# A Flamingo block on one core: query and key stacks written from PSUM by column-repeated fp32r weights, and all later keys and values projected in the prologue

## The reference, cut to what matters

```python
for L in range(4):
    x = x + tanh(g_xattn[L]) * xattn[L](layernorm(x), ctx)
    x = x + tanh(g_ffn[L]) * ffn[L](layernorm(x))
# xattn[1]: q = n @ Wq.T + bq; k = ctx @ Wk.T + bk; v = ctx @ Wv.T + bv
#           softmax(q k^T / sqrt(8)) v per head, then @ Wo.T + bo
# xattn[2]: no biases, no scale; one key and value head of 8 features shared by all 16 heads;
#           only keys with |key - query| <= 32 (NEG elsewhere)
# xattn[3]: as 1, and where(mask == 0, -10000, scores) ahead of the softmax
```

## Time and profile before

| what | value |
|---|---|
| runs | 831.49, 822.17 and 829.42 us, median 829.42 |
| span of the profiled execution | 829.3 us |
| PE busy | 651.2 us, 79% |
| VectorE busy | 551.9 us, 67% |
| ScalarE busy | 365.6 us, 44% |
| GpSimd busy | 297.9 us, 36% |
| DMA queue, share of 16 engines | 17.2% |
| instructions | 12053 |
| shares of the chain of waits | PE 66%, DVE 17%, DMA 8%, ACT 4%, issue 3% |

### The profile page before, as it was taken

The page is one execution under the profiler, slowest core; times in us unless marked ns, Lnnn a source line. Parts: engine busy times, 40 slices in busy tenths (PEclk is TensorE's granted clock), DMA queues, the critical chain, the costliest instruction groups (busy, mean ns, idle before and its releaser), DMA issues.

```text
span 829.3 us, 12053 instructions
## 1 busy us (share of the span) xinstructions
PE 651.2 (79%) x3570; PEld 421.2 (51%) x3570; DVE 551.9 (67%) x1490; ACT 365.6 (44%) x642; POOL 297.9 (36%) x551
## 2 busy tenths in 40 slices
PE   4347699962898787982699976999994399975997
PEld 4235477741345465751255553677763044444675
DVE  2785788873675438874567436788886478835686
ACT  1102345421467423431166632677773055641575
POOL 2963246621221242630111141567662011102463
PEclk9776599985699757995599985899997589985799
DMA  7000011255100200155300100111135500000011
GB/s 254 0 1 0 0 30 48 48 59 65 21 4 3 64 1 10 49 66 60 38 3 3 29 0 1 32 40 39 44 53 63 63 3 3 3 26 0 21 44 39
DMA packets 25339, 27.55 MB, mean 33 GB/s; under 512 B 4483, under 2 KB 23750, under 8 KB 25286
## 3 DMA queue, kind: packets, MB, share of 16 engines
q1 hardware_dynamic: 25286, 26.90, 17.2%
HBM read 16.63 MB, written 0.52 MB: 21 GB/s over the span
## 4 chain that ended last, share of the span: by engine, by line
PE 66%; DVE 17%; DMA 8%; ACT 4%; issue 3%; SPq 1%; POOL 1%; DVEq 0%; ACTq 0%; POOLq 0%
PE PS L547 10%; PE PS L548 10%; PE PS L549 9%; PE PS L721 5%; PE PS L704 5%; PE PS L675 5%; DMA qst<-qp 5%; PE PS L569 4%; PE PS L701 4%; DVE xn L979 2%; DMA qst<-nmT 2%; PE PS L734 1%; PE PS L635 1%; PE PS L468 1%; PE PS L634 1%
## 5 line engine op out<-in xcount | busy, mean ns | idle before, releaser
L329 POOL TENSOR_TENSOR wpair<-ring,ones_col 128x128 fp32r<-128x128 f32 (+1 forms) x150 | 78.0, 520 | 161.4 <-PE PS L549 131.1
L916 ACT ACTIVATE pT<-PS 128x512 f32<-128x512 f32 x192 | 110.8, 598 | 45.0 <-PE PS L704 40.0
L1160 DVE TENSOR_TENSOR pT<-pT,PS 128x512 f32<-128x512 f32 x150 | 102.4, 684 | 38.3 <-ACT pT L847 31.2
L675 PE MATMUL PS<-kst,qst 96*128 96x256 bf16 x384 | 85.4, 311 | 42.7 <-DMA qst<-qp 37.3
L1166 DVE TENSOR_TENSOR hid_lo<-pT,hid_hi 128x512 fp32r<-128x512 f32 x150 | 110.6, 738 | 2.4 <-ACT hid_hi L854 1.4
L331 POOL TENSOR_TENSOR wpair<-ring,wpair 128x128 fp32r<-128x128 f32 (+1 forms) x150 | 104.3, 695 | 11.8
L854 ACT ACTIVATE hid_hi<-pT 128x512 fp32r<-128x512 f32 x150 | 93.5, 623 | 15.8 <-DVE pT L1160 15.3
L547 PE MATMUL PS<-hid_hi,wpair 128*128 128x512 f32 x150 | 87.3, 582 | 4.1 <-DVE hid_lo L1166 4.1
L547 PE MATMUL PS<-xhi,wpair 128*128 128x512 f32 x204 | 88.0, 431 | 1.9 <-DVE pT L1160 1.1
L548 PE MATMUL PS<-xlo,wpair 128*128 128x512 f32 x204 | 84.6, 415 | 0.0
L847 ACT ACTIVATE pT<-PS,ring 128x512 f32<-128x512 f32 x96 | 66.0, 690 | 42.0 <-PE PS L549 42.0
(11 more groups left out here) (210 smaller groups left out, 1171.0 us busy)
## 6 DMA issues: line engine op xcount, KB each, us to landing
ring<-in_mlp SPq DMA_DIRECT2D x48, 128.5 KB, 2.0
ring<-in_glu SPq DMA_DIRECT2D x27, 192.0 KB, 2.4
kst<-kp SPq DMA_DIRECT2D x36, 128.0 KB
qst<-qp SPq DMA_DIRECT2D x36, 128.0 KB
qst<-nmT SPq DMA_DIRECT2D x96, 3.0 KB
att_w<-in_att_w SPq DMA_DIRECT2D x4, 257.0 KB, 8.2
consts<-in_consts SPq DMA_DIRECT2D x1, 988.5 KB, 5.6
x_res<-in_x SPq DMA_DIRECT2D x1, 512.0 KB, 3.7
```

Source lines behind the costliest of these rows:

```text
L675: mm = pe.matmul(PS[:, v % 2, j * S:(j + 1) * S], qst[0:KROWS, h0 + j, b * S + q * P:b * S + (q + 1) * P], kst[0:KROWS, h0 + j, b * S:(b + ...
L916: act.activation(pT[:, w % 8, :], PS[:, 2 + w % 2, :], ACT.Exp, scale=sc).then_inc(A["p"], 1)
L1160: dve.tensor_tensor(hid[:, hf, :], src[:, hf, :], PS[:, 6 + hf, :], ALU.mult).then_inc(M["hid"], 1)
```

## The change

**The stacks.** Queries and keys are no longer split in three bf16 parts. The weights are repeated by column, so that one projection writes for four heads (32 rows each) the rows: the 8 features three times, and 8 rows more of which two are used. `stacked(w)` on the host makes them. A stack is now in fp32r with 24 rows for a head (`SROWS`), 26 with the two rows for the maximum (`MROWS`), and head h lies in rows 32 (h % 4) on and in group h // 4 (`HGRP` = 4 groups). The three blocks of 8 rows are to hold high, rest and high part; ACT copies with a sign or zero for each row (`take_queries`), and VectorE adds the rest where it belongs (`finish_queries`); for keys two ACT copies and a POOL addition (`complete_keys`). The score matmuls use 24 or 26 rows, a tile of 32 of the array's 128 rows. The mask matmul stays one over 128 rows, the value matmul stays one of 128 rows and 32-column tiles with 9 columns in place of 32 (`vall` has 9).

**Queries.** Four projections for each half, of three fp32r matmuls of 512 columns each; in layers 1 and 3 a fourth one with two rows (`ones2`, `brow`) adds the bias. Those of the second half lie inside the loop at p = 4, 5, 8 and 9 (`Q_AT`). No DMAs fill the stacks; those of `nmT` stay (two for four units, 8 partitions).

**Keys and values** of layers 1 to 3 are projected in the prologue in 23 chunks (`chunks`), split over four places by `KV_AT`: 4 behind layer 0's value projection, 4 behind the query transform, 9 behind the correlation, 6 at the end. Context and key weights are split in two fp32r parts there by ACT and POOL. `kst` exists for each layer. POOL's five memsets of the stacks and `split_keys` go. The mask's loads stand ahead of the experts' weights on SP.

**The maxima.** A unit's two score matmuls are now one head's two query tiles, and not two heads'. `split_maxima` makes two fp32r parts with two operations and not four; `turn_max` is two fp32 transposes and not one in bf16. `LAG` is 14.

The core of the diff:

```diff
-PAIRS = ((0, 0), (0, 1), (1, 0), (1, 1), (0, 2), (2, 0))
-QUERY_ORDER = sorted(enumerate(PAIRS), key=lambda pair: pair[1][0])
-KROWS = 96
-SROWS = KROWS + PARTS
+HGRP = 4
+SROWS = 3 * HD
+MROWS = SROWS + 2
...
-        LAG = 12
+        LAG = 14
         NU = B * H
+        Q_AT = (4, 5, 8, 9)
+        KV_AT = (4, 8, 14, 17)
...
+        chunks = ([("k", 1, hf, a) for hf in range(NHALF) for a in range(HGRP)] + [("v", 1, hf, 0) for hf in range(NHALF)]
+                  + [("k", 2, hf, 0) for hf in range(NHALF)] + [("v", 2, 0, 0)]
+                  + [("k", 3, hf, a) for hf in range(NHALF) for a in range(HGRP)] + [("v", 3, hf, 0) for hf in range(NHALF)])
...
-            def stack_keys(L):
-                if L == 1:
-                    sp.wait_ge(stacks_set, 7)
-                else:
-                    sp.wait_ge(at["p"], (L - 1) * NU)
-                for hf in range(NHALF):
-                    sp.wait_ge(at["kparts"], (L - 1) * adds["kparts"] + hf + 1)
-                    for n, (_, g) in enumerate(PAIRS):
-                        sp.dma_start(kst[n * HD:(n + 1) * HD, :, hf * HALF:(hf + 1) * HALF],
-                                     kp[:, g, hf * HALF:(hf + 1) * HALF]).then_inc(at_kst[L][hf], 16)
 
...
-                        sp.dma_start(qst[n * HD:(n + 1) * HD, :, hf * HALF:(hf + 1) * HALF],
-                                     qp[:, g, hf * HALF:(hf + 1) * HALF]).then_inc(at_qst[L][hf], 16)
...
-                        sp.dma_start(qst[KROWS:SROWS, 4 * g:4 * g + 4, b * S + q * P:b * S + (q + 1) * P],
-                                     nmT[q * PARTS * 4:(q + 1) * PARTS * 4, G, :]).then_inc(at_nmd[g], 16)
+                    for part in range(2):
+                        sp.dma_start(qst[SROWS + part:P:32, a, b * S:(b + 1) * S].bitcast(f32),
...
-            stacks(((kst, 32, 0.0), (kst, 64, 0.0), (kst, 96, ones_pair), (qst, 32, 0.0), (qst, 64, 0.0)), 2)
-            pool.wait_ge(stacks_set, 7)
+            split_key_weights(1)
+            split_context()
+            split_key_weights(2)
+            split_key_weights(3)
+            complete_keys(0, KV_AT[3])
             layer_norm(1)
+            complete_keys(KV_AT[3], len(chunks))
             split_weights(0, True)
             for L in range(1, 4):
...
+                if kind == "k":
+                    c, w = slice(hf * HALF, (hf + 1) * HALF), wkpair[L][:, :, a * P:(a + 1) * P]
+                    pe.wait_ge(wk_split[L], 2)
+                    pe.matmul(o, w[:, 0, :], chi[:, c], start=True, stop=False)
+                    pe.matmul(o, w[:, 0, :], clo[:, c], start=False, stop=False)
+                    mm = pe.matmul(o, w[:, 1, :], chi[:, c], start=False, stop=True)
...
-            def project_keys(L):
-                pe.wait_ge(ld_att[L], 32 if L == 2 else 48)
-                for hf in range(NHALF):
-                    pe.matmul(PS[:, hf, :], W[:, P:2 * P], ctxT[:, hf * HALF:(hf + 1) * HALF],
-                              start=True, stop=True).then_inc(at["k"], 1)
-                if L > 1:
-                    pe.wait_ge(at["on"], (L - 1) * adds["on"])
-                    pe.wait_ge(at["fin_e"], (L - 1) * adds["fin_e"])
-                else:
-                    pe.wait_ge(ac["voe"], 1)
-                for i in range(NT):
-                    o = PS[:, 6 + i // 4, (i % 4) * P:(i % 4 + 1) * P]
-                    pe.matmul(o, ctxT[:, i * P:(i + 1) * P], W[:, 2 * P:3 * P], start=True, stop=False)
-                    mm = pe.matmul(o, ones_row[:, :], row[:, 0:P], start=False, stop=True)
...
-                                       qst[0:KROWS, h0 + j, b * S + q * P:b * S + (q + 1) * P],
-                                       kst[0:KROWS, h0 + j, b * S:(b + 1) * S], start=True, stop=True)
+                    for q in range(TB):
+                        mm = pe.matmul(PS[:, v % 2, q * S:(q + 1) * S],
+                                       queries_of(h)[0:SROWS, b * S + q * P:b * S + (q + 1) * P],
...
+                def project_queries(hf, a, bank):
+                    c, w = slice(hf * HALF, (hf + 1) * HALF), wqpair[:, :, a * P:(a + 1) * P]
+                    if a == 0:
+                        pe.wait_ge(ln_xlo, NHALF * (2 * L - 1) + hf + 1)
+                    if hf == 0 and a == 0:
                         pe.wait_ge(wq_split, 2 * L)
-                    c = slice(hf * HALF, (hf + 1) * HALF)
-                    pe.matmul(PS[:, 2 + hf, :], wqpair[:, 0, :], xhi[:, c], start=True, stop=False)
-                    pe.matmul(PS[:, 2 + hf, :], wqpair[:, 0, :], xlo[:, c], start=False, stop=False)
-                    pe.matmul(PS[:, 2 + hf, :], wqpair[:, 1, :], xhi[:, c], start=False, stop=True).then_inc(A["q"], 1)
+                    if hf == 1:
+                        pe.wait_ge(A["qe"], pre["qe"] + a + 3)
+                    pe.matmul(PS[:, bank, :], w[:, 0, :], xhi[:, c], start=True, stop=False)
+                    pe.matmul(PS[:, bank, :], w[:, 0, :], xlo[:, c], start=False, stop=False)
+                    mm = pe.matmul(PS[:, bank, :], w[:, 1, :], xhi[:, c], start=False, stop=(L == 2))
+                    if L != 2:
+                        r = (L // 2) * WIDE + a * P
+                        mm = pe.matmul(PS[:, bank, :], brow[:, r:r + P], ones2[:, :], start=False, stop=True)
...
-                    pe.transpose(PS[0:TB * PARTS * 4, 6, 0:64].bitcast(bf16),
-                                 nmpart[:, G, :, :, :].rearrange("p q a n -> p (q a n)"), identb[:, :]).then_inc(A["nmt"], 1)
+                    for q in range(TB):
+                        mm = pe.transpose(PS[0:2 * HGRP, 6, q * P:(q + 1) * P],
+                                          nmpart[:, G, q, :, :].bitcast(f32).rearrange("p a n -> p (a n)"), ident)
...
-                                       kst[0:SROWS, h, b * S + k * P:b * S + (k + 1) * P],
-                                       qst[0:SROWS, h, b * S:(b + 1) * S], start=(L == 1), stop=True,
+                                       keys_of(h)[:, b * S + k * P:b * S + (k + 1) * P],
+                                       queries_of(h)[:, b * S:(b + 1) * S], start=(L == 1), stop=True,
...
-                            mm = pe.matmul(PS[32 * j:32 * j + 32, 4 + g // 2, (g % 2) * S:(g % 2 + 1) * S],
-                                           vall[:, TB * b + k, h, :], pT[:, (H * b + h) % 8, k * S:(k + 1) * S],
+                            mm = pe.matmul(PS[32 * j:32 * j + 9, 4 + g // 2, (g % 2) * S:(g % 2 + 1) * S],
+                                           vall[L][:, TB * b + k, 0 if L == 2 else h, :], pT[:, (H * b + h) % 8, k * S:(k + 1) * S],
...
+                    if p in Q_AT:
+                        project_queries(1, Q_AT.index(p), 4 + Q_AT.index(p) % 2)
...
+                if kind == "k":
+                    dst, col = kst[L][:, a, hf * HALF:(hf + 1) * HALF], KB_COL[L] + a
+                    act.activation(dst, PS[:, 6 + n % 2, :], ACT.Identity, scale=consts[:, C_SGN:C_SGN + 1],
+                                   bias=kbs[:, col:col + 1])
+                    if k >= 2:
+                        act.wait_ge(k_ready, k - 1)
...
+                def take_queries(hf, a, bank):
+                    act.wait_ge(A["q"], pre["q"] + HGRP * hf + a + 1)
+                    act.activation(qst[:, a, hf * HALF:(hf + 1) * HALF], PS[:, bank, :], ACT.Copy,
+                                   scale=consts[:, C_SGN + 2:C_SGN + 3]).then_inc(A["qt"], 1)
...
-                    link(dve.scalar_tensor_tensor(out=rest[:, :], in0=PS[:, 2 + hf, :], scalar=att_w[L][:, 4 * P:4 * P + 1],
-                                                  in1=qp[:, 0, c], op0=ALU.add, op1=ALU.subtract))
-                    link(dve.tensor_copy(qp[:, 1, c], rest[:, :]))
-                    dve.tensor_tensor(qp[:, 2, c], rest[:, :], qp[:, 1, c], ALU.subtract).then_inc(done, 1)
-                    dve.wait_ge(done, pre["qparts"] + hf + 1)
...
+                def finish_queries(hf, a, bank):
+                    dst = qst[:, a, hf * HALF:(hf + 1) * HALF]
+                    dve.wait_ge(A["qt"], pre["qt"] + HGRP * hf + a + 1)
+                    dve.scalar_tensor_tensor(out=dst, in0=PS[:, bank, :], scalar=consts[:, C_SGN + 3:C_SGN + 4],
+                                             in1=dst.bitcast(f32), op0=ALU.mult, op1=ALU.add).then_inc(A["qe"], 1)
...
-                        dve.tensor_reduce(negmax[:, b, q, h0:h0 + 2], PS[:, v % 2, :].rearrange("p (h k) -> p h k", h=2),
+                        dve.tensor_reduce(negmax[:, b, :, h], PS[:, v % 2, :].rearrange("p (q k) -> p q k", q=TB),
```

More of the change, by code:

```diff
@@ L88, in build @@
         identb = sb("identb", [P, P], bf16)
-        ones_row = sb("ones_row", [1, P])
         ones_col = sb("ones_col", [P, 1])
@@ L182, in build @@
         ld_att = [sem(f"ld_att{L}") for L in range(4)]
+        ld_out = [None] + [sem(f"ld_out{L}") for L in range(1, 4)]
         ld_route = sem("ld_route")
@@ L496, in autocorrelation @@
                 mm.then_inc(ac["vo"], 1)
+                for n in range(0, KV_AT[0]):
```

(7 more changed lines are left out.)

389 lines of the change are left out of this document (215 added, 174 removed).

## The result

| | before | changed |
|---|---|---|
| runs of this comparison | 831.49, 822.17, 829.42, 828.78 | 965.85, 964.94, 957.3, 965.51 |
| median, us | 829.10 | 965.23 |
| span of the profiled execution, us | 829.3 | 964.1 |
| PE busy | 651.2 us, 79% | 817.6 us, 85% |
| share of the chain of waits: PE, DMA | 66%, 8% | 77%, 1% |

The changed kernel takes 1.164 times as long (95% interval 1.157 to 1.171). The forecast was 962. The mechanism is the one that was forecast, but the nearness of the total is partly luck: the loops came out 20 us cheaper than the sum said, and the gains 20 us smaller.

What follows compares the result with a forecast made beforehand. The prediction took the loop over 64 heads as TensorE's, with DMA between query projection and first scores; at the slow clock with overlap, 829.3 + 173 (loops) - 40 (gains) = 962 us, range 885 to 1020.

Steps and rivals of the forecast that it cites:

- the loops: Head loops of layers 1 to 3: +24.4 us in layer 1, +74.2 each in layers 2 and 3, sum +173.
- the gains: Savings outside the loops' groups: stacks -21, keys and values -13, prologue -6 us, sum -40.
- The clock: All three head loops: few-row scores keep TensorE at 1.2 GHz, granted 0.50; rival of full clock, 809 us, chance 0.15.
- Layer 3 enters at full clock, groups of 1.2: Layer 3, first query copy to first shifted scores: 3.5 + 2.5 + 15 = 21 us against 33.4, -12.
- Switches: Layers 2 and 3, scores to mask and back: 0.14 + 0.30 = 0.44 us a head that did not exist.
- Overlap: Score matmuls in different 32-row groups run together; groups 5.15 and 8.97 us; rival without overlap 994 us, chance 0.30.
- Three output transposes a layer at the slow clock (+2.5): Head loops: this cost cancels with the slow start the loop already has today (-2.5).
- The tails: Last 14 heads, without maxima, 3.5 groups: layer 1 3.9 us against some 3.1; layers 2 and 3 7.35 against some 3.7.
- What was gained: the stacks: First query copy to first shifted scores: -1, -8 and -12 us in layers 1 to 3, together -21.
- 14 heads at VectorE's pace: Layer 2, before the first shifted scores: VectorE paces 14 heads at 0.75 us, within 20.4 us against 28.8.
- What was gained: keys and values: Between output projection and next transposes VectorE's norm sets the pace, 5.3 us: -8 and -5, together -13.
- What was gained: the prologue: Five POOL memsets go, 23 chunks come in: -6 us, between -12 (all hidden) and +8.

Runs made afterwards that it cites:

- experiment 1: Changed kernel plus 16 extra bf16 matmuls over 128 rows behind the first value group of each layer's loop: 931.23 us, 1.125 times the kernel before.
- experiments 1 and 2: Changed kernel plus 16 extra matmuls behind each layer's first value group, over 128 rows in the first (931.23 us), over 24 rows in the second (989.18 us).
- experiment 5: Changed kernel with the mask matmuls of two heads made one behind the other in layers 2 and 3: 907.84 us, one run.
- experiment 6: Changed kernel with the output transposes and VectorE's normalising behind them two heads later: 948.39 us, one run.

## Why the prediction was right, and where not

**The clock.** The step came out: 0.50 in all three loops up to the last maximum scores. Its price is shown by experiment 1, where a group of the same kernel takes 4.63 us at 1.00 and 8.01 at 0.50. Its reason, the rows of the array, is shown only for the extra matmuls of experiments 1 and 2; with LAG 16 and with mask pairs the same 24-row scores had 1.00 for 61 us and for over 30 us of layers 2 and 3. So that the whole of all three loops is slow is in part luck. That PE enters each loop slow is right too. The term "Layer 3 enters at full clock, groups of 1.2" is wrong. The projections of its first half and the transposes behind them, in the changed kernel:

```profile
701.90:711.30 9.40, 9.40 (x20) 0.50 0.00 0
```

The clock is 0.50 ahead of the first query copy at 703.5 us, so that layer 3 took 29.1 us from first copy to first shifted scores where 21 stood in the sum.

**Switches.** 0.44 us a head forecast, 0.40 measured, but the parts are the other way round: 0.30 was to stand behind the mask and 0.14 ahead of it; in the timeline above the scores start 0.53 us behind the mask of 0.43, and the next mask 0.73 behind scores of 0.43, so 0.10 and 0.30.

**Overlap.** Taken as there, and it is, but mis-sized: I counted three slots for four scores in layers 2 and 3, it is two. A group is 8.01 and not 8.97 us: over 12.5 groups, 12 us less in each of the two layers. In layer 1 it is 5.37 against 5.15.

**The output transposes.** This step failed. "Three output transposes a layer at the slow clock (+2.5)" was to cancel with the slow start. They cost 4.6 us in layer 2 and 5.9 in layer 3 over a plain group, three times a layer, against 1.5 in layer 2 of the kernel before (two groups of 4.73 and 4.88 us in place of 4.06 hold them there): the slow clock doubles the transposes, and the new wait stands behind them. I had looked at what LAG did to the overlap and to the start, and not at what then stood directly behind the transposes in PE's queue.

**The tails.** Layers 1 and 2 were cheaper than forecast, since the clock came back to 1.00 for a part of them once the maximum scores had gone; in layer 3 it did not (0.50 from 860 to 876 us). The tails of layers 1 and 2:

```profile
290.00:305.00 15.00, 13.05 (x107) 0.73 0.20 55
545.00:560.00 15.00, 11.62 (x90) 0.95 0.00 1
```

From first shifted scores to the end of the last values the three layers take 89.0, 130.1 and 139.9 us, against 61.9, 70.8 and 72.9: +27, +59 and +67, together +153 in place of +173.

**What was gained: the stacks.** From first query copy to first shifted scores: 27.2, 24.4 and 29.1 us against 27.6, 29.2 and 33.9, so -0.4, -4.9 and -4.8 where -1, -8 and -12 stood; the query stage ahead of the copy took back 2. The step that failed in layer 2 is "14 heads at VectorE's pace". The chain of waits of the changed kernel:

```profile
409.77 0.72 PE PS L681
410.50 0.43 PE PS L682
410.93 0.43 PE PS L683
411.35 0.72 PE PS L708 x2
```

A projection inside the loop and its unit of scores are 2.3 us of PE, at the slow clock and with a switch on either side, and four of them pace the start while VectorE waits. The 36 DMAs are gone, and what replaced them is nearly as long. The first maximum scores of layer 2 do start early, 4.3 us behind the first query copy where 11 was forecast, but that gains nothing, since the four projections stand behind them.

**What was gained: keys and values.** To the second half's transposes -7.0 and -3.6 us against -8 and -5. Right.

**What was gained: the prologue.** -6 forecast; the transposes of layer 0's second norm start at 81.30 and 81.23 us, so nothing. VectorE's eight norm operations went to 5.78 us, and VectorE had the lags 11.0 us earlier than before (its operation on them starts at 50.99 and 61.99). Chunks took it back. First, ScalarE's exponential of the lags stood behind them, and VectorE waited for it, in its timeline:

```profile
56.09 0.17 DVE L1108 TENSOR_REDUCE pT<-pT 128x4 f32<-128x20 f32 x1 [4.92 <-ACT pT L987]
```

I had let VectorE's chain cover the nine chunks behind the correlation, and had not seen that a link of that chain, the exponential, runs on the engine that takes the chunks out. Another 3.1 us went behind it: three VectorE forms (L1110, L1114, L1118) took 4.5 us where they take 1.4 before, while GpSimd's additions for the chunks ran beside them. The last 3 us went in the six chunks at the end, where the value matmuls waited 3.2 us for ScalarE's key copies.

In all: +153 in the loops, -8 for the stacks, -11 for keys and values, nothing in the prologue, and some +1 elsewhere make +135, where +173 - 40 = +133 was forecast. Two errors of 20 us cancelled.

## What to carry to other kernels

Before a matmul is put on fewer rows, look at what that does to the granted clock of the whole stage, not only at its columns: here the order of a unit stayed the same and the clock halved, for a gain on DMAs that were only 8% of the chain. Look in a profile for one-row or other small-tile matmuls between full ones, and put them together. When a lag or an order is changed, read again what stands directly behind each instruction that hands a bank to another engine.

## What the runs showed of the hardware that was not expected

Four fp32r matmuls in two row groups of 32 start in pairs 0.01 us apart, even where both of one group were issued first (443.82 and 443.83 above). Six in three row groups take as long as two (0.73 us, experiment 5). A clock that has risen stays up through scores of 24 rows for 17 to 27 us behind sixteen dense matmuls (experiment 1) and for 3.5 us in experiment 6, and is lost in one place (749 us, experiment 1) with PE busy in all of the 20 us ahead. A fill of 32 partitions by 8192 columns on GpSimd takes 6.9 us, and a VectorE cast that took 0.22 us elsewhere took 6.41 behind it.
